# 64-row score products and q picks, and value products behind the half step, in a four-layer transformer kernel

## The chip, the cores and the metric

One NeuronCore of one Trainium2 chip runs the whole program in one launch. The metric is the device time of that core in microseconds (us), the median of three runs.

## The reference, cut to what matters

Sixteen sequences of 512 tokens with 512 features pass through four layers, each behind a layer norm and with a residual: a delta-rule attention, a feed-forward layer with a top-2 LoRA, a softmax attention with a linear memory, and the feed-forward layer again. The change lies in the third layer:

```python
qh = q.reshape(b, s, N_QUERY, N_HEAD, D_HEAD)      # 4 x 8 = 32 heads of 16 features
kh = k.reshape(b, s, N_HEAD, D_HEAD)               # 8 key/value heads
scores = jnp.einsum('bsqhd,bthd->bqhst', qh, kh) * scale
probs = jax.nn.softmax(scores, axis=-1)
a_dot = jnp.einsum('bqhst,bthd->bsqhd', probs, vh)
sigma_q = jax.nn.elu(q.reshape(b, s, N_QUERY, D_KV))
a_mem = sigma_q @ memory / (sigma_q @ memory_norm)
out = a_dot * (1.0 - w) + a_mem * w
```

## The kernel before

The program has two parts, one after the other. `delta_rule_layer` does the first layer of all sequences, some 2.8 ms; `token_layers` does the other three, one sequence after another (16 passes of a loop body that is unrolled twice), some 227 us each. The change touches `token_layers` alone.

In its attention the scores are needed twice. Once with the queries on the partitions, to find each query's maximum (`maximum(g, st)`, called M below: head g, query tile st of 128): TensorE writes 128 x 512 scores into one of three PSUM banks, and VectorE reduces them to one column (`tensor_reduce`, line 1586). Once with the keys on the partitions (`score(h, tt)`, called S: head h, key tile tt): TensorE writes them into one of three other banks, with the maximum already taken off, and ScalarE takes the exponential into `probs` (line 1140). Both products are float32r matmuls of 512 columns. A head has only 16 features, split in parts that are stacked: 48 rows of products and one row for the shift, in a block of 64 rows. `q_stack` holds two heads per tile, the even one in rows 0 to 63 and the odd one in rows 64 to 127. `k_stack` holds one tile for each of the 8 key heads, with zeros in the 64 rows of the other parity, so that a contraction over all 128 rows gives one head. The zeros are made by the scale and bias columns `head_rows` in `k_pair` (VectorE for pairs 0 and 2, ScalarE for 1 and 3, two instructions for each pair).

The stacks are made by selection products: `pick_k` (lines 1248 and 1249, a hi and a lo product of 32 rows each, from another 32-row block for each pair) and `pick_q(m)` (lines 1275 and 1276, a hi and a lo product of 128 rows, where only 32 rows of `sel` aren't zero), each copied out by `k_pair` or by ScalarE's `q_pair`.

The order on TensorE is written out by hand. Step g of 45 has two half steps j. In each stands, as far as it applies: up to two q picks (g below 7), M(g, 2j), at j = 1 of every fourth step four transposes of the maxima (line 1360, called maxT, which become the shift), S(g-7, 2j), a value block, M(g, 2j+1), S(g-7, 2j+1), and the products with the memory (line 1290). The value block (`values`, line 1333, called V) is one key tile of four heads: four plain float32 matmuls, 128 rows by 32 columns each, side by side. Four heads make a quad and have four value blocks, in the half steps that `AV_SLOTS` names: j = 1 of steps 4n+3, 4n and 4n+1 (V0 to V2), j = 0 of step 4n+2 (V3). At the end of every fourth step (4n+3) the finished quad is transposed (line 1380, called turn), VectorE normalises it (lines 1576 and 1580) ahead of its next maximum, and the next maxT waits for that, since both use bank 7.

The order of the others follows. ScalarE takes the exponentials in order; the first one of head h (h of 7 and more) waits for `av_mm`, that is for the last value block of the quad whose `probs` buffer it overwrites. M waits for the reduction three before it, S for the exponential three before it, and TensorE works off its queue in order. The first 7 to 8 steps have maxima and picks (called stretch A), steps up to 31 have maxima and scores (B), steps 32 to 38 scores alone (C), and then come the last value blocks.

Of the kernel before, what the change touches and what calls it, by code (L numbers as in the profile page):

```python
# [18 lines left out]
F32R = mybir.dt.float32r  # L19
# [4 lines left out]
P = 128  # L24
# [816 lines left out]
def token_layers(nc, dims, x2_in, w_ffn, b_ffn, lora_b, gate_b, w_q, w_kv, mem_aug_in, mem_w_in, ident_in, rank_mask_in, sel_in, head_rows_in, out):  # L841
# [3 lines left out]
    with ExitStack() as ctx:  # L845
        def sb(name, shape, dt=F32):
            return ctx.enter_context(nc.sbuf_tensor(name, shape, dt))
# [29 lines left out]
        sel = sb("sel", [P, 2 * HP + 2, P], F32R)  # L877
        head_rows = sb("head_rows", [P, 2, 2])

# [14 lines left out]
        q_stack = sb("q_stack", [P, NQ * NKV // 2, SEQ], F32R)  # L895
        k_stack = sb("k_stack", [P, NKV, SEQ], F32R)
        v_aug = sb("v_aug", [P, NT, NKV, 32])
# [151 lines left out]
        def _(act):  # L1049
# [4 lines left out]
            act.wait_ge(c_in, 112)  # L1054
            act.activation(mem_w[:, :], mem_w[:, :], ACT.Tanh, scale=0.5).then_inc(mem_tanh, 1)

            def norm_hi(b, f):
# [5 lines left out]
            with act.Fori(0, NBATCH // 2) as bb:  # L1063
                for par in range(2):
# [30 lines left out]
                    def k_pair(m):  # L1095

                        act.wait_ge(ksel_mm, at(b, HP, m + 1))
                        for e in range(2):
                            last = act.activation(k_stack[:, 2 * m + e, :], ps[:, m % STACK_BANKS, :], ACT.Identity,
                                                  bias=head_rows[:, e, 1:2], scale=head_rows[:, e, 0:1])  # L1100
                        last.then_inc(kodd_ready, 1)

# [57 lines left out]
        def _(pe):  # L1160
# [23 lines left out]
            with pe.Fori(0, NBATCH // 2) as bb:  # L1184
                for par in range(2):
# [84 lines left out]
                    def pick_q(m):  # L1270
                        n, hp = divmod(m, HP)
                        if hp == 0:
                            pe.wait_ge(qlo_ready, at(b, NQ, n + 1))
                        bank = stack_bank(HP + m)
                        pe.matmul(ps[:, bank, :], sel[:, hp, :], q_hi[:, n, :], start=True, stop=False)  # L1275
                        pe.matmul(ps[:, bank, :], sel[:, HP + hp, :], q_lo[:, n, :], start=False, stop=True).then_inc(qsel_mm, 1)  # L1276

# [16 lines left out]
                    def pair(h):  # L1294

                        n, kv = divmod(h, NKV)
                        return n * HP + kv // 2, kv

                    def maximum(g, st):

                        qt, kv = pair(g)
                        m = NT * g + st
                        if m in (1, 2):
                            pe.wait_ge(qrelu_ready, at(b, NQ, m))
                            pe.wait_ge(qlo_ready, at(b, NQ, m))
                        elif m >= MAX_BANKS:
                            pe.wait_ge(max_ready, at(b, NT * NH, m - MAX_BANKS + 1))
                        pe.matmul(ps[:, STACK_BANKS + m % MAX_BANKS, :], q_stack[:, qt, P * st:P * st + P], k_stack[:, kv, :],  # L1308
                                  start=True, stop=True).then_inc(max_mm, 1)

                    def score(h, tt):

                        qt, kv = pair(h)
                        if h == 0 and tt == 0:
                            pe.wait_ge(qstack_ready, at(b, NQ * HP, NQ * HP))
                        if h % 4 == 0 and tt == 0:
                            pe.wait_ge(shift_in, at(b, 64 * QUADS, 64 * (h // 4 + 1)))
                        m = NT * h + tt
                        if m >= STACK_BANKS:
                            pe.wait_ge(exp_ready, at(b, NT * NH, m - STACK_BANKS + 1))  # L1320
                        pe.matmul(ps[:, m % STACK_BANKS, :], k_stack[:, kv, P * tt:P * tt + P], q_stack[:, qt, :],  # L1321
                                  start=True, stop=True).then_inc(score_mm, 1)
# [15 lines left out]
                    for g in range(NH + OUT_LAG):  # L1338
                        h = g - SCORE_LAG
                        for j in range(2):  # L1340
# [21 lines left out]
                            if 0 <= h < NH:  # L1362
                                score(h, 2 * j)
                            quad, i = divmod(g - 3 - AV_LAG, 4)
                            if (i, j) in AV_SLOTS and 0 <= quad < QUADS:
                                values(quad, AV_SLOTS.index((i, j)))
                            if g < NH:
                                maximum(g, 2 * j + 1)
                            if 0 <= h < NH:
                                score(h, 2 * j + 1)  # L1370
                            if j == 0 and 0 <= g - MEM_LAG < NT:
                                memory(g - MEM_LAG)
# [15 lines left out]
        def _(dve):  # L1388
# [11 lines left out]
            dve.wait_ge(dve_consts, 2)  # L1400
            dve.wait_ge(c_in, 112)
            dve.wait_ge(pool_consts, 3)
            dve.wait_ge(w_hi_done, 5)
# [45 lines left out]
            with dve.Fori(0, NBATCH // 2) as bb:  # L1449
                for par in range(2):  # L1450
# [86 lines left out]
                    def k_pair(m):  # L1537

                        dve.wait_ge(ksel_mm, at(b, HP, m + 1))
                        for e in range(2):  # L1540
                            last = dve.tensor_scalar(k_stack[:, 2 * m + e, :], ps[:, m % STACK_BANKS, :], head_rows[:, e, 0:1], head_rows[:, e, 1:2],
                                                     ALU.mult, ALU.add)
                        last.then_inc(keven_ready, 1)

# [134 lines left out]
```

## Time and profile before

| | us |
|---|---|
| median of 3 runs (lowest, highest) | 6420.12 (6418.07, 6423.28) |
| the profiled execution's own time | 6432.57 |
| its span | 6430.8 |
| TensorE matmuls busy | 5567.4 (87%) |
| VectorE busy | 3720.7 (58%) |
| ScalarE busy | 2422.5 (38%) |
| GpSimd busy | 909.5 (14%) |
| mean granted TensorE clock | 0.836 of full |

### The profile page before, as it was taken

How to read it: one execution, taken by the hardware profiler on the slowest of the kernel's cores; microseconds unless marked ns; L12 is line 12 of the kernel's file. 1: busy time of each engine (PE TensorE's matmuls, PEld its weight loads, DVE VectorE, ACT ScalarE, POOL GpSimd, SP SyncE). 2: the span in 40 equal slices, each digit the busy share in tenths (PEclk: the TensorE clock that was granted, in tenths of full speed). 3: DMA queues.
4: the chain of work that ended last, by engine and by line, in shares of the span. 5: the costliest groups of instructions: out<-in, count | busy, mean ns of one | idle time of the engine just before them, and what ended most of it. 6: DMA issues, size and time to landing. Idle time of an engine off the chain costs nothing.

```text
span 6430.8 us, 154830 instructions
## 1 busy us (share of the span) xinstructions
PE 5567.4 (87%) x62928; PEld 4184.4 (65%) x62928; DVE 3720.7 (58%) x7900; ACT 2422.5 (38%) x4497; POOL 909.5 (14%) x1075
## 2 busy tenths in 40 slices
PE   4899888889888988859889988988898899889888
PEld 4788787778777888745655565555556555555655
DVE  3555555555555555526756665665566567566656
ACT  2222222222222222216435534544554454345345
POOL 0111111111111111111111121112112111210111
PEclk8777776777777777669999989999999999899899
DMA  2111111111111111110000000000000000000000
GB/s 62 43 46 44 43 45 49 49 48 49 49 49 42 46 44 43 45 54 1 14 14 14 1 15 14 1 15 14 15 1 14 15 1 14 14 14 1 15 14 8
DMA packets 352479, 173.53 MB, mean 27 GB/s; under 512 B 300016, under 2 KB 300784, under 8 KB 350992
## 3 DMA queue, kind: packets, MB, share of 16 engines
q1 hardware_dynamic: 343056, 146.25, 8.5%
q10 hardware_dynamic: 8704, 16.78, 0.8%
q8 instruction: 562, 9.21, 0.6%
q14 instruction: 157, 1.29, 0.1%
HBM read 94.27 MB, written 67.63 MB: 25 GB/s over the span
## 4 chain that ended last, share of the span: by engine, by line
issue 27%; PE 19%; DVE 6%; POOL 3%; ACT 1%; DMA 0%; DVEq 0%; POOLq 0%; SPq 0%; ACTq 0%
PE row_psum L40 5%; PE row_psum L42 4%; PE row_psum L41 4%; DVE smax L1586 2%; POOL xs L1042 1%; PE row_psum L1171 1%; PE row_psum L1308 1%; DVE stats L1412 1%; PE row_psum L1275 1%; POOL rstd L1014 1%; PE row_psum L1276 1%; PE row_psum L1290 1%; DVE xr_lo L1441 0%; DVE xs L1515 0%; DVE probs L1423 0%
## 5 line engine op out<-in xcount | busy, mean ns | idle before, releaser
L1586 DVE TENSOR_REDUCE smax<-row_psum 128x1 f32<-128x512 f32 x2048 | 1279.5, 683 | 306.9 <-PE row_psum L1308 305.9
L1140 ACT ACTIVATE probs<-row_psum 128x512 f32<-128x512 f32 x2048 | 1109.1, 602 | 505.2 <-PE row_psum L1321 401.2
L1308 PE MATMUL row_psum<-k_stack,q_stack 128*128 128x512 f32 x2048 | 872.4, 437 | 28.2 <-DVE smax L1586 24.5
L1321 PE MATMUL row_psum<-q_stack,k_stack 128*128 128x512 f32 x2048 | 837.2, 423 | 22.3 <-ACT probs L1140 13.8
L1308 PEld LDWEIGHTS row_psum<-k_stack,q_stack 128*128 128x128 f32 x2048 | 394.5, 193 | 462.1 <-DVE smax L1586 388.3
L529 PE MATMUL span_bank<-rhs,inv_b 32*32 32x64 f32 x8192 | 441.8, 303 | 150.0 <-issue 84.3
L1333 PE MATMUL row_psum<-probs,v_aug 128*32 128x512 f32 x4096 | 538.9, 604 | 9.2 <-ACT av_sb L1153 9.2
L1321 PEld LDWEIGHTS row_psum<-q_stack,k_stack 128*128 128x128 f32 x2048 | 380.3, 191 | 254.3 <-ACT probs L1140 198.0
L529 PEld LDWEIGHTS span_bank<-rhs,inv_b 32*32 32x32 f32 x8192 | 424.0, 166 | 160.4 <-issue 160.4
L708 DVE TENSOR_TENSOR lane_t<-lane_t,lane_p 128x30 f32<-128x30 f32 (+14 forms) x960 | 408.6, 426 | 33.0
L723 DVE TENSOR_TENSOR tri<-span_bank,masks 128x512 f32<-128x512 f32 x256 | 156.0, 682 | 383.1 <-PE span_bank L509 383.1
L40 PE MATMUL row_psum<-wf_hi,xr_hi 128*128 128x320 f32 (+1 forms) x1024 | 335.4, 328 | 31.9 <-issue 17.7
L705 DVE TENSOR_TENSOR lane_p<-lane_t 128x30 f32<-128x30 f32 (+14 forms) x960 | 340.0, 354 | 30.8
L41 PE MATMUL row_psum<-wf_lo,xr_hi 128*128 128x320 f32 (+1 forms) x1024 | 331.9, 324 | 0.0
L42 PE MATMUL row_psum<-wf_hi,xr_lo 128*128 128x320 f32 (+1 forms) x1024 | 331.5, 324 | 0.0
L1171 PE MATMUL row_psum<-ident,probs 128*128 128x128 f32 x784 | 167.5, 368 | 177.5 <-DVE probs L1423 177.5
L1042 POOL TENSOR_TENSOR xs<-xs,av_n 128x256 f32<-128x256 f32 x128 | 93.1, 727 | 1549.7 <-DVE av_n L1580 1549.7
L40 PE MATMUL span_bank<-x_hi,w_hi 128*128 128x256 f32 x1024 | 299.0, 292 | 3.0 <-DVE x_lo L687 3.0
L732 DVE TENSOR_TENSOR rhs<-rhs,span_bank 128x512 f32<-128x512 f32 x128 | 82.3, 684 | 364.4 <-PE span_bank L529 364.4
L41 PE MATMUL span_bank<-x_lo,w_hi 128*128 128x256 f32 x1024 | 287.6, 281 | 0.0
L42 PE MATMUL span_bank<-x_hi,w_lo 128*128 128x256 f32 x1024 | 287.2, 281 | 0.0
L1171 PEld LDWEIGHTS row_psum<-ident,probs 128*128 128x128 f32 x784 | 117.7, 184 | 226.3 <-DVE probs L1423 176.1
(203 smaller groups left out, 10609.0 us busy)
## 6 DMA issues: line engine op xcount, KB each, us to landing
xs<-x SPq DMA_DIRECT2D x17, 1024.0 KB, 5.6
x_sp<-in_x ACTq DMA_DIRECT2D x32, 512.0 KB, 3.3
tri_dram<-tri SPq DMA_DIRECT2D x256, 64.0 KB, 2.3
lane_t<-tri_dram SPq DMA_DIRECT2D x32, 512.0 KB, 3.4
inv_dram<-lane_t SPq DMA_DIRECT2D x32, 512.0 KB, 2.6
inv_b<-inv_dram SPq DMA_DIRECT2D x256, 64.0 KB, 2.3
x_res<-in_x SPq DMA_DIRECT2D x32, 512.0 KB, 4.5
x<-x_res SPq DMA_DIRECT2D x32, 512.0 KB, 2.8
```

Source lines behind the costliest of these rows:

```text
L40: pe.matmul(out, a_hi, b_hi, start=first, stop=False)
L41: pe.matmul(out, a_hi, b_lo, start=False, stop=False)
L42: return pe.matmul(out, a_lo, b_hi, start=False, stop=last)
L529: last = pe.matmul(bank[4 + 2 * t + h // 8][dst:dst + NB, 2 * HD * (h % 8):2 * HD * (h % 8) + 2 * HD], weights(h, src), moving(src, h), st ...
L705: mark(dve.tensor_tensor(prod, lane_t[:, 0:m, m:m + 1].to_broadcast([P, m, n]), lane_t[:, m:m + 1, m + 1:NB].to_broadcast([P, m, n]), ALU. ...
L708: mark(dve.tensor_tensor(lane_t[:, 0:m, m + 1:NB], lane_t[:, 0:m, m + 1:NB], prod, ALU.add))
L1140: act.activation(probs[:, h % PROBS, tt, :], ps[:, m % STACK_BANKS, :], ACT.Exp, scale=float(DH) ** -0.5).then_inc(exp_ready, 1)
L1171: last = pe.transpose(ps[:, t, P * k:P * k + P], xn[:, t, P * k:P * k + P], ident2[:, :])
L1308: pe.matmul(ps[:, STACK_BANKS + m % MAX_BANKS, :], q_stack[:, qt, P * st:P * st + P], k_stack[:, kv, :], start=True, stop=True).then_inc(m ...
L1321: pe.matmul(ps[:, m % STACK_BANKS, :], k_stack[:, kv, P * tt:P * tt + P], q_stack[:, qt, :], start=True, stop=True).then_inc(score_mm, 1)
L1333: last = pe.matmul(ps[32 * e:32 * e + 32, 6, :], v_aug[:, tt, h % NKV, :], probs[:, h % PROBS, tt, :], start=tt == 0, stop=tt == NT - 1)
L1586: dve.tensor_reduce(smax[:, g, st:st + 1], ps[:, STACK_BANKS + (NT * g + st) % MAX_BANKS, :], AX.X, ALU.max).then_inc(max_ready, 1)
```

## The change

`k_stack` gets one tile for a pair of key heads, the even in rows 0 to 63 and the odd in rows 64 to 127, without zeros; `k_pair` becomes one instruction for each pair, which adds a column of ones in the two shift rows (`shift_ones`, made once at the start, for which ScalarE and VectorE wait once). `maximum` and `score` contract over the 64 rows of their head, taken from both stacks. `pick_q` contracts over the 64 rows in which its selection lies. And the value block stands behind the second M and S of its half step, no longer between the first S and the second M.

```diff
@@ -876,6 +876,7 @@
 
         sel = sb("sel", [P, 2 * HP + 2, P], F32R)
         head_rows = sb("head_rows", [P, 2, 2])
+        shift_ones = sb("shift_ones", [P, 1])
 
 
         xs = sb("xs", [P, 2, NT, D])
@@ -893,7 +894,7 @@
         xat_hi = sb("xat_hi", [P, SEQ], F32R)
         xat_lo = sb("xat_lo", [P, SEQ], F32R)
         q_stack = sb("q_stack", [P, NQ * NKV // 2, SEQ], F32R)
-        k_stack = sb("k_stack", [P, NKV, SEQ], F32R)
+        k_stack = sb("k_stack", [P, HP, SEQ], F32R)
         v_aug = sb("v_aug", [P, NT, NKV, 32])
         smax = sb("smax", [P, NQ * NKV, NT])
         shift = sb("shift", [4, SEQ], F32R)
@@ -1053,6 +1054,7 @@
                 act.activation(d2, stage[:, 0:size], ACT.Copy).then_inc(w_hi_done, 1)
             act.wait_ge(c_in, 112)
             act.activation(mem_w[:, :], mem_w[:, :], ACT.Tanh, scale=0.5).then_inc(mem_tanh, 1)
+            act.wait_ge(dve_consts, 3)
 
             def norm_hi(b, f):
                 for t in range(NT):
@@ -1095,10 +1097,8 @@
                     def k_pair(m):
 
                         act.wait_ge(ksel_mm, at(b, HP, m + 1))
-                        for e in range(2):
-                            last = act.activation(k_stack[:, 2 * m + e, :], ps[:, m % STACK_BANKS, :], ACT.Identity,
-                                                  bias=head_rows[:, e, 1:2], scale=head_rows[:, e, 0:1])
-                        last.then_inc(kodd_ready, 1)
+                        act.activation(k_stack[:, m, :], ps[:, m % STACK_BANKS, :], ACT.Identity,
+                                       bias=shift_ones[:, 0:1]).then_inc(kodd_ready, 1)
 
                     def q_pair(m):
                         act.wait_ge(qsel_mm, at(b, NQ * HP, m + 1))
@@ -1272,8 +1272,9 @@
                         if hp == 0:
                             pe.wait_ge(qlo_ready, at(b, NQ, n + 1))
                         bank = stack_bank(HP + m)
-                        pe.matmul(ps[:, bank, :], sel[:, hp, :], q_hi[:, n, :], start=True, stop=False)
-                        pe.matmul(ps[:, bank, :], sel[:, HP + hp, :], q_lo[:, n, :], start=False, stop=True).then_inc(qsel_mm, 1)
+                        r = slice(64 * (hp // 2), 64 * (hp // 2) + 64)
+                        pe.matmul(ps[:, bank, :], sel[r, hp, :], q_hi[r, n, :], start=True, stop=False)
+                        pe.matmul(ps[:, bank, :], sel[r, HP + hp, :], q_lo[r, n, :], start=False, stop=True).then_inc(qsel_mm, 1)
 
                     pick_q(0)
 
@@ -1294,23 +1295,24 @@
                     def pair(h):
 
                         n, kv = divmod(h, NKV)
-                        return n * HP + kv // 2, kv
+                        e = kv % 2
+                        return n * HP + kv // 2, kv // 2, slice(64 * e, 64 * e + 64)
 
                     def maximum(g, st):
 
-                        qt, kv = pair(g)
+                        qt, hp, rows = pair(g)
                         m = NT * g + st
                         if m in (1, 2):
                             pe.wait_ge(qrelu_ready, at(b, NQ, m))
                             pe.wait_ge(qlo_ready, at(b, NQ, m))
                         elif m >= MAX_BANKS:
                             pe.wait_ge(max_ready, at(b, NT * NH, m - MAX_BANKS + 1))
-                        pe.matmul(ps[:, STACK_BANKS + m % MAX_BANKS, :], q_stack[:, qt, P * st:P * st + P], k_stack[:, kv, :],
+                        pe.matmul(ps[:, STACK_BANKS + m % MAX_BANKS, :], q_stack[rows, qt, P * st:P * st + P], k_stack[rows, hp, :],
                                   start=True, stop=True).then_inc(max_mm, 1)
 
                     def score(h, tt):
 
-                        qt, kv = pair(h)
+                        qt, hp, rows = pair(h)
                         if h == 0 and tt == 0:
                             pe.wait_ge(qstack_ready, at(b, NQ * HP, NQ * HP))
                         if h % 4 == 0 and tt == 0:
@@ -1318,7 +1320,7 @@
                         m = NT * h + tt
                         if m >= STACK_BANKS:
                             pe.wait_ge(exp_ready, at(b, NT * NH, m - STACK_BANKS + 1))
-                        pe.matmul(ps[:, m % STACK_BANKS, :], k_stack[:, kv, P * tt:P * tt + P], q_stack[:, qt, :],
+                        pe.matmul(ps[:, m % STACK_BANKS, :], k_stack[rows, hp, P * tt:P * tt + P], q_stack[rows, qt, :],
                                   start=True, stop=True).then_inc(score_mm, 1)
 
                     def values(quad, tt):
@@ -1361,13 +1363,13 @@
                                 last.then_inc(maxT_mm, 1)
                             if 0 <= h < NH:
                                 score(h, 2 * j)
-                            quad, i = divmod(g - 3 - AV_LAG, 4)
-                            if (i, j) in AV_SLOTS and 0 <= quad < QUADS:
-                                values(quad, AV_SLOTS.index((i, j)))
                             if g < NH:
                                 maximum(g, 2 * j + 1)
                             if 0 <= h < NH:
                                 score(h, 2 * j + 1)
+                            quad, i = divmod(g - 3 - AV_LAG, 4)
+                            if (i, j) in AV_SLOTS and 0 <= quad < QUADS:
+                                values(quad, AV_SLOTS.index((i, j)))
                             if j == 0 and 0 <= g - MEM_LAG < NT:
                                 memory(g - MEM_LAG)
                         quad, i = divmod(g - 3 - TURN_LAG, 4)
@@ -1399,6 +1401,8 @@
             dve.tensor_scalar(mem_w[:, :], mem_w[:, :], 0.5, 0.5, ALU.mult, ALU.add).then_inc(dve_consts, 1)
             dve.wait_ge(dve_consts, 2)
             dve.wait_ge(c_in, 112)
+            dve.tensor_tensor(shift_ones[:, :], head_rows[:, 0, 1:2], head_rows[:, 1, 1:2], ALU.add).then_inc(dve_consts, 1)
+            dve.wait_ge(dve_consts, 3)
             dve.wait_ge(pool_consts, 3)
             dve.wait_ge(w_hi_done, 5)
             own = [0]
@@ -1537,10 +1541,8 @@
                     def k_pair(m):
 
                         dve.wait_ge(ksel_mm, at(b, HP, m + 1))
-                        for e in range(2):
-                            last = dve.tensor_scalar(k_stack[:, 2 * m + e, :], ps[:, m % STACK_BANKS, :], head_rows[:, e, 0:1], head_rows[:, e, 1:2],
-                                                     ALU.mult, ALU.add)
-                        last.then_inc(keven_ready, 1)
+                        dve.tensor_scalar(k_stack[:, m, :], ps[:, m % STACK_BANKS, :], shift_ones[:, 0:1], None,
+                                          ALU.add).then_inc(keven_ready, 1)
 
                     def elu_exp(n):
 

```

## Rows read from the trace of the kernel before

**Rows 1.** The page's costliest groups: count, then busy us and mean ns, idle before.

```profile
L1586 DVE TENSOR_REDUCE smax<-row_psum 128x1 f32<-128x512 f32 x2048 | 1279.5, 683 | 306.9 <-PE row_psum L1308 305.9
L1140 ACT ACTIVATE probs<-row_psum 128x512 f32<-128x512 f32 x2048 | 1109.1, 602 | 505.2 <-PE row_psum L1321 401.2
L1308 PE MATMUL row_psum<-k_stack,q_stack 128*128 128x512 f32 x2048 | 872.4, 437 | 28.2 <-DVE smax L1586 24.5
L1333 PE MATMUL row_psum<-probs,v_aug 128*32 128x512 f32 x4096 | 538.9, 604 | 9.2 <-ACT av_sb L1153 9.2
```

**Rows 2.** A stretch: length, busy PE, PEld, DVE, ACT, POOL (counts); PEclk, DMA share, GB/s.

```profile
3165.60:3232.90 67.30, 67.21 (x363) 35.08 (x362) 53.02 (x90) 47.73 (x91) 2.91 (x4) 1.00 0.01 2
```

**Rows 3.** Timeline of VectorE, one quad: start us, us, instruction, idle before.

```profile
3193.30 1.88 DVE L1586 TENSOR_REDUCE smax<-row_psum 128x1 f32<-128x512 f32 x3
3195.93 2.48 DVE L1586 TENSOR_REDUCE smax<-row_psum 128x1 f32<-128x512 f32 x4 [0.75 <-PE row_psum L1308]
3198.97 1.29 DVE L1586 TENSOR_REDUCE smax<-row_psum 128x1 f32<-128x512 f32 x2 [0.55 <-PE row_psum L1308]
3201.09 3.68 DVE L1586 TENSOR_REDUCE smax<-row_psum 128x1 f32<-128x512 f32 x6 [0.83 <-PE row_psum L1308]
3205.40 0.69 DVE L1586 TENSOR_REDUCE smax<-row_psum 128x1 f32<-128x512 f32 x1 [0.63 <-PE row_psum L1308]
...
3206.70 1.88 DVE L1586 TENSOR_REDUCE smax<-row_psum 128x1 f32<-128x512 f32 x3
```

**Rows 4.** Timeline of TensorE's matmuls, same quad.

```profile
3196.89 0.39 PE L1308 MATMUL row_psum<-k_stack,q_stack 128*128 128x512 f32 x1
3197.12 0.39 PE L1321 MATMUL row_psum<-q_stack,k_stack 128*128 128x512 f32 x1
3197.43 1.06 PE L1333 MATMUL row_psum<-probs,v_aug 128*32 128x512 f32 x8
3198.43 0.50 PE L1308 MATMUL row_psum<-k_stack,q_stack 128*128 128x512 f32 x1
3198.77 0.39 PE L1321 MATMUL row_psum<-q_stack,k_stack 128*128 128x512 f32 x1
...
3205.44 0.60 PE L1380 MATMUL row_psum<-ident,av_sb 128*128 128x128 f32 x4
3205.79 0.48 PE L1308 MATMUL row_psum<-k_stack,q_stack 128*128 128x512 f32 x1
```

**Rows 5.** Timeline of TensorE's matmuls, around the first three k picks.

```profile
3115.53 0.51 PE L1248 MATMUL row_psum<-xat_hi,sel 32*128 32x512 f32 x3
3115.87 0.40 PE L1249 MATMUL row_psum<-xat_lo,sel 32*128 32x512 f32 x3
3116.20 0.50 PE L40 MATMUL row_psum<-xr_hi,wq_hi 128*128 128x512 f32 x1
```

**Rows 6.** Timeline of TensorE's weight loads, a maximum that waited for its bank.

```profile
3202.43 0.19 PEld L1308 LDWEIGHTS row_psum<-k_stack,q_stack 128*128 128x128 f32 x1 [0.19 <-DVE smax L1586]
```

**Rows 7.** Timeline of ScalarE, behind V3 of the same quad.

```profile
3200.75 1.17 ACT L1140 ACTIVATE probs<-row_psum 128x512 f32<-128x512 f32 x2 [0.95 <-PE row_psum L1333]
3201.82 0.59 ACT L1153 ACTIVATE av_sb<-row_psum 128x512 f32<-128x512 f32 x1
3202.29 2.57 ACT L1140 ACTIVATE probs<-row_psum 128x512 f32<-128x512 f32 x5
```

**Rows 8.** Stretches of 5 us, columns as in rows 2.

```profile
2010.00:2015.00 5.00, 5.00 (x104) 5.00 (x102) 1.28 (x2) 0.18 (x1) 0.00 (x0) 0.50 0.00 0
...
3155.00:3160.00 5.00, 4.21 (x14) 3.34 (x15) 3.12 (x6) 2.73 (x5) 1.28 (x1) 0.66 0.00 0
...
3240.00:3245.00 5.00, 4.39 (x20) 1.88 (x20) 0.03 (x1) 4.46 (x9) 0.00 (x0) 1.00 0.01 2
```

**Rows 9.** Timeline of VectorE, at the start of stretch B.

```profile
3157.89 0.69 DVE L1586 TENSOR_REDUCE smax<-row_psum 128x1 f32<-128x512 f32 x1 [0.16 <-PE row_psum L1308]
```

**Rows 10.** Timeline of ScalarE, set-up, behind the last q projection.

```profile
3122.98 1.09 ACT L1093 ACTIVATE xr_hi<-row_psum 128x512 fp32r<-128x512 f32 x2 [1.24 <-PE row_psum L42]
```

## Prediction, made before the changed kernel ran

> **What bounds the kernel now.** I read the page's groups first. In `token_layers` the costliest are the maxima, their reductions, the exponentials and the value blocks. VectorE sits idle 306.9 us ahead of its 2048 reductions, nearly all of it waiting for M, ScalarE 505.2 us ahead of the exponentials, most of it for S, while TensorE waits 28.2 us ahead of M [rows 1]. So in this attention TensorE sets the pace. Next I asked where. In one sequence's stretch with maxima, scores and value blocks, from 3165.60 to 3232.90, TensorE is busy 67.21 of 67.30 us at clock 1.00, VectorE 53.02 and ScalarE 47.73 [rows 2]. That leaves VectorE 14.3 us idle; over 16 sequences 228 us, the ceiling of a gain here.
>
> The timelines of one quad give the period and its parts. The quad takes 3206.70 - 3193.30 = 13.40 us. Reductions that aren't held up follow each other every 0.60 us (four in 2.48, the last record 0.69). The normalisation adds 3206.70 - 3205.40 - 0.69 = 0.61. VectorE thus needs 16 x 0.60 + 0.61 = 10.2 us, and loses 3.2 in four gaps of 0.55 to 0.83 [rows 3]. On TensorE M to S is 0.23 us. Around a value block S to V is 0.31, V to M 1.00 and M to S 0.34, in all 1.65 where two slots would be 0.46: a block costs 1.19. The turn costs 0.35 [rows 4], maxT is alike. Sum: 32 x 0.23 + 4 x 1.19 + 2 x 0.4 = 12.9, with short waits 13.4. TensorE bound.
>
> **The change part by part.**
>
> *64-row products.* M of head g and S of head g-7 lie always in opposite halves of the rows, since 7 is odd. Can they run side by side? The three k picks of 32 rows, each in its own row block, show it: their three hi matmuls begin within one record of 0.51 us, the three lo ones 0.34 later, and the next product 0.33 after that. Six matmuls take 0.67 us; in line they would take 6 x 0.23 = 1.4 [rows 5]. So row blocks do overlap, in this number format. Picks wait for no semaphore between them, M and S do; that is the part not shown. Bounds for a pair M, S: 0.23 (full overlap) and 0.46 (none). I take 0.23, by the nearest row. TensorE's quad is then 16 x 0.23 + 4 x 1.19 + 1.2 (turn and maxT with their changes of shape) = 9.6 us, below VectorE's 10.2. The bound moves to VectorE and to how the blocks interrupt it.
>
> *What is late next.* M may go once the reduction three before is over: 0.69 after that one's start plus 0.05 (a reduction that began at about 3201.69 lets the weight load go at 3202.43 [rows 6]), so 0.74. From M with its weight load to the reduction's start it is 3198.97 - 3198.43 = 0.54. Three reductions last 1.80, so M has 1.80 - 0.74 - 0.54 = 0.52 us of slack. A value block behind a pair: 0.11 for the pair's weight load (M to S behind a block is 0.34, not 0.23), 0.31 to V, 1.00 to the next M: 1.42, where 0.60 + 0.52 = 1.12 is free of cost. VectorE idles 0.3 us for each of V1, V2 and V3. V0 is followed at once by the turn, for whose end VectorE's normalisation waits: turn at 1.42, over at 2.02, while VectorE would be free at 1.66: 0.4. V3 now stands behind the second S, and the first exponential of the next head waits for V3. Already ScalarE waits 0.95 for it [rows 7]. Behind V3 ScalarE has five exponentials and the copy (3201.82 to 3202.29 is 0.47, the exponentials 0.51 each) before it gives the bank that the S ahead of V0 needs: 5 x 0.51 + 0.47 + 0.14 = 3.2 us, where VectorE's pace would want that S 2.5 behind V3. So V0 starts 0.7 late, and VectorE pays it. Idle in a quad 0.9 + 0.4 + 0.7 = 2.0, with a repeated hold-up at V2 to V3 (only four maxima apart less two) 2.1: quad 12.3 us instead of 13.4. The stretch holds 67.3 / 13.4 = 5.0 quads: 5.5 us a sequence. Bounds of this term: 0 (no overlap) and 14.3 (all idle gone).
>
> *Position of V in stretch C.* No maxima are left there, ScalarE's order sets the pace, and S of one head can't overlap its own kind (same half). V3 comes one S later, 0.23 us, and ScalarE waits for it: twice, -0.5 us. Bounds: -1 and 0.
>
> *Start of B.* The clock is 0.66 in mean there [rows 8], and VectorE waits 0.16 before each reduction, 0.85 apart, since M and S take 0.43 each [rows 9]. Three such gaps go when they overlap: +0.5. Bounds 0 and 1.
>
> *k_pair.* Two fewer instructions each on VectorE and ScalarE, about 1.5 us a sequence and engine. Worth nothing: TensorE's q projections run on meanwhile, and ScalarE has waited 1.24 us for the last of them before it takes q over [rows 10]. The same cover holds the one constant and its wait at the start. If that cover were gone it would give up to 1.5 a sequence.
>
> *q picks.* The rows of the contraction don't shorten a matmul. Some picks now fall in the other half than their neighbour M. Stretch A is bound by VectorE apart from its first steps: 0, bounds -1 (below) and +1.
>
> *Changes of shape.* S to V is 0.31 against 0.23 between equal shapes, and the first after a change loads its weights uncovered, 0.11 [rows 4]: 0.1 to 0.2 for each change. New are two around each maxT and each memory block and one at each turn, some 32 a sequence. Most fall where VectorE or ScalarE sets the pace: those at turn and maxT are in the 9.6 above; elsewhere 0.2 a sequence, bounds 0 and 5.
>
> The Trainium skill ("TensorEngine Tiling (Array Packing)", Key Properties) says that changing the tiling mode drains the engine; this speaks against the change where it adds such changes, and the 0.31 against 0.23 agrees with it. By that rule alone the sum stays, as the drain is in the row's price.
>
> *Clock.* In the delta layer TensorE is busy 5.00 of 5.00 us with 32 x 32 tiles, and the granted clock is 0.50 [rows 8]. So being busy isn't enough; parts of the array seem to count less. In stretch C the clock holds at 1.00 with full-row scores and value blocks [rows 8]; it will have 64-row scores there, and in A 64-row maxima and picks. What would one fall cost? A value block's 1.00 us would be 1.87 (0.43 / 0.23), so 0.87 for each block that is caught, and in A next to nothing for M and picks, which have slack, some 0.3 for a step. Bounds 0 and 14 (half of the 32 blocks). I take two blocks caught in a sequence and a step of A: -2.0 us.
>
> The Trainium skill ("TensorE: Matmul & The Clock Gate", Why this matters for your kernels) asks only for no long pauses between matmuls; by that the clock term would be 0 and the sum 85 us instead of 53. The row of the delta layer doesn't agree with it, so I keep the term.
>
> Sum per sequence: 5.5 - 0.5 + 0.5 - 0.2 - 2.0 = 3.3 us, times 16 = 53 us. The profiled execution took 6432.57 us, span 6430.8; it would take 6380. The median of the runs is 12.45 lower, which I carry over: 6367.
>
> **Rivals.**
>
> 1. *The blocks are hidden better.* If ScalarE's chain behind V3 doesn't reach V0 and the clock holds: idle in a quad 1.3, quad 11.5, 1.9 x 5 = 9.5 a sequence, 152 us: 6268; with one of the two alone some 6320. For it: ScalarE needs only 47.73 of 67.30 us [rows 2]. Against: it waits for V3 by a fixed order [rows 7]. I name 6300.
>
> 2. *The clock falls (slower).* Half-array matmuls leave TensorE at 1.2 GHz for much of the attention. Place: every value block caught there, price 0.87 each. Gains without the clock are 5.3 a sequence, so from 6 caught blocks of 32 the change loses. At 9 blocks: 7.8 + 1.0 in A = 8.8, net -3.5, times 16 = 56: 6476. For it: clock 0.50 at full busy in the delta layer. Against: value blocks and overlapped pairs fill the whole array, and C holds 1.00 now with S only every 0.51 us [rows 8].
>
> 3. *M and S don't overlap*, because each waits for its own semaphore, so the change doesn't do what it could. The quad stays 13.4 plus three changes of shape, 0.5, and the later V3: 5 x 0.5 + 0.5 = 3.0 a sequence, at most: 6420 to 6468. Against it the picks [rows 5].
>
> **How the numbers follow.** My forecast (6340 to 6405 by itself) has a chance of 0.60, rival 1 0.20, rival 2 0.14, rival 3 0.06. Range: from between rival 1 and its end, 6280, to 6440, which leaves out the bulk of rival 2. About 0.2%, 13 us, can be told from no change. Faster: 0.48 of the forecast and all of rival 1, 0.68. Within 0.2%: 0.12 of the forecast (a clock term of some 5) and 0.02 each of the others, 0.16. Slower: 0.12 and 0.04, 0.16.
>
> **What would show it.** The profile after should show M and S starting within 0.15 us of each other, a quad of about 12.3 us, VectorE waiting behind V and the turn rather than between, and ScalarE still waiting for V3, longer than 0.95. TensorE's stretch B should be no longer all busy. The windows of A and C tell the clock term: at 1.00 throughout rival 1 is nearer, below 0.8 rival 2. If starts of M and S stay 0.23 apart, the main step is wrong.

## The result and the profile after

The changed kernel takes 6565.62 us (6547.28 to 6590.44, 4 runs) beside 6421.70 before (4 runs): a ratio of 1.0225, 95% interval [1.0204, 1.0245]. It is 144 us slower; the forecast was 53 us faster. The profiled execution took 6561.14 us, span 6559.3, mean granted clock 0.788 where it was 0.836.

The page's groups of the changed kernel, as in [rows 1]:

```profile
L1588 DVE TENSOR_REDUCE smax<-row_psum 128x1 f32<-128x512 f32 x2048 | 1273.6, 683 | 211.8 <-PE row_psum L1310 209.7
L1140 ACT ACTIVATE probs<-row_psum 128x512 f32<-128x512 f32 x2048 | 1073.1, 613 | 608.4 <-PE row_psum L1323 353.8
L1310 PE MATMUL row_psum<-k_stack,q_stack 64*128 64x512 f32 x2048 | 905.8, 518 | 49.3 <-DVE smax L1588 43.2
L1335 PE MATMUL row_psum<-probs,v_aug 128*32 128x512 f32 x4096 | 622.3, 690 | 5.9 <-ACT av_sb L1153 5.9
```

VectorE waits 95 us less for the maxima. But most of that comes back at the turn. Its wait ahead of the reciprocal of the normalisation, first before, then after:

```profile
L1576 DVE RECIPROCAL av_rc<-row_psum 128x16 f32<-128x16 f32 x128 | 33.0, 258 | 376.6 <-PE row_psum L1380 376.6
L1578 DVE RECIPROCAL av_rc<-row_psum 128x16 f32<-128x16 f32 x128 | 33.0, 257 | 620.3 <-PE row_psum L1382 620.3
```

All idle time of VectorE inside stretch B together went from 236 to 206 us, so the gain is there, but it is 30 us. ScalarE waits 103 us more, and a record of a value product lasts 690 ns instead of 604, one of a maximum 518 instead of 437, though none has more columns. Matmuls that get longer without more work point to the clock.

Next, TensorE's matmuls in an undisturbed quad of the changed kernel:

```profile
3198.34 1.06 PE L1335 MATMUL row_psum<-probs,v_aug 128*32 128x512 f32 x8
3199.34 0.66 PE L1382 MATMUL row_psum<-ident,av_sb 128*128 128x128 f32 x4
3199.92 0.49 PE L1310 MATMUL row_psum<-k_stack,q_stack 64*128 64x512 f32 x1
3199.93 0.49 PE L1323 MATMUL row_psum<-q_stack,k_stack 64*128 64x512 f32 x1
3200.26 0.39 PE L1310 MATMUL row_psum<-k_stack,q_stack 64*128 64x512 f32 x1
3200.26 0.39 PE L1323 MATMUL row_psum<-q_stack,k_stack 64*128 64x512 f32 x1
```

M and S start within 0.01 us of each other, where they stood 0.23 apart [rows 4]. They overlap fully, although each has its own wait for a semaphore. V0 and the turn stand one behind the other, and the next maximum comes 1.58 us behind V0's start. VectorE in the same quad, and ScalarE behind V3:

```profile
3187.72 2.48 DVE L1588 TENSOR_REDUCE smax<-row_psum 128x1 f32<-128x512 f32 x4
3190.79 2.48 DVE L1588 TENSOR_REDUCE smax<-row_psum 128x1 f32<-128x512 f32 x4 [0.59 <-PE row_psum L1310]
3193.50 1.29 DVE L1588 TENSOR_REDUCE smax<-row_psum 128x1 f32<-128x512 f32 x2 [0.23 <-PE row_psum L1310]
3195.15 3.69 DVE L1588 TENSOR_REDUCE smax<-row_psum 128x1 f32<-128x512 f32 x6 [0.36 <-PE row_psum L1310]
3200.03 0.26 DVE L1578 RECIPROCAL av_rc<-row_psum 128x16 f32<-128x16 f32 x1 [1.20 <-PE row_psum L1382]
...
3200.67 2.47 DVE L1588 TENSOR_REDUCE smax<-row_psum 128x1 f32<-128x512 f32 x4
```

```profile
3194.81 1.08 ACT L1140 ACTIVATE probs<-row_psum 128x512 f32<-128x512 f32 x2 [1.93 <-PE row_psum L1335]
```

The quad takes 12.95 us (3200.67 - 3187.72) against 13.40 [rows 3]; most other quads at full clock take 12.82. VectorE waits 0.2 to 0.6 behind the blocks and 1.20 for the turn; ScalarE's wait for V3 is 1.93 instead of 0.95 [rows 7].

Then the stages of one sequence, first before, then after. The four rows are stretch A (to the first maximum of step 7), steps 7 to 10, stretch B from step 11 to the last maximum, and C with the last value blocks; columns as in [rows 2]:

```profile
3126.59:3149.08 22.49, 19.83 (x83) 13.58 (x83) 20.80 (x39) 11.51 (x21) 2.97 (x3) 0.94 0.01 1
3149.08:3163.31 14.23, 11.58 (x51) 8.30 (x49) 12.19 (x26) 8.12 (x16) 3.38 (x3) 0.88 0.01 2
3163.31:3232.23 68.92, 68.83 (x370) 35.36 (x369) 54.22 (x93) 48.79 (x93) 2.91 (x4) 1.00 0.01 2
3232.23:3258.58 26.35, 23.42 (x137) 8.46 (x135) 2.72 (x8) 17.38 (x33) 2.18 (x3) 1.00 0.01 1
```

```profile
3116.72:3143.09 26.37, 23.98 (x85) 16.51 (x83) 20.94 (x40) 11.01 (x20) 3.50 (x3) 0.56 0.01 1
3143.09:3156.78 13.69, 10.91 (x47) 7.28 (x46) 11.98 (x25) 7.64 (x16) 2.83 (x3) 0.75 0.01 2
3156.78:3225.80 69.02, 65.41 (x365) 25.07 (x366) 54.00 (x92) 47.40 (x93) 2.90 (x4) 0.92 0.01 2
3225.80:3263.72 37.92, 34.98 (x145) 11.33 (x144) 2.69 (x9) 17.18 (x34) 2.19 (x3) 0.70 0.01 1
```

The clock is 0.56 in A and 0.70 in C, where it was 0.94 and 1.00, though TensorE is busy for no smaller share: 91% of A (23.98 of 26.37) after 88%, 92% of C after 89%. In C the same value blocks take 1.94 us each, where one took 1.06 before [rows 4]:

```profile
3245.12 1.94 PE L1335 MATMUL row_psum<-probs,v_aug 128*32 128x512 f32 x8
3246.99 2.27 PE L1323 MATMUL row_psum<-q_stack,k_stack 64*128 64x512 f32 x4
3249.19 1.94 PE L1335 MATMUL row_psum<-probs,v_aug 128*32 128x512 f32 x8
```

To see all sequences, I took from each trace the starts of the 1st, 29th, 45th and 128th reduction and of the last reciprocal of every sequence. The means over the sequences in us, with the time at 1.2 GHz in brackets ("rest" is all else of a sequence, of which there are 15 intervals):

```
                A             7 to 10       B             C             rest
before          22.44 ( 2.4)  13.72 (1.9)   68.99 (0.0)   26.36 ( 0.0)  92.12
after           25.08 (19.8)  13.55 (6.0)   66.80 (6.0)   35.14 (16.0)  92.13
v_move          22.53 ( 2.6)  14.25 (3.6)   69.81 (0.0)   29.89 ( 3.0)  91.83
rows_only       25.09 (19.9)  13.55 (6.0)   65.23 (1.9)   32.85 (16.2)  91.96
b_only_vold     22.27 ( 1.8)  13.75 (6.6)   66.60 (5.5)   26.29 ( 0.0)  91.95
b_only_vnew     22.40 ( 2.2)  13.69 (6.5)   68.30 (9.3)   29.96 ( 3.0)  91.89
c64             22.54 ( 2.7)  14.04 (3.0)   68.97 (0.0)   28.52 ( 5.1)  91.62
a64             36.11 (31.1)  14.39 (3.4)   68.95 (0.0)   26.37 ( 0.0)  91.67
picks64         35.37 (30.2)  14.72 (4.8)   69.00 (0.0)   26.37 ( 0.0)  91.86
c_shadow        25.91 (22.0)  13.63 (5.9)   66.92 (6.2)   29.88 ( 1.9)  91.07
b11             22.29 ( 1.7)  13.87 (2.3)   64.49 (0.0)   26.30 ( 0.0)  91.62
b11_mix         22.26 ( 1.7)  14.02 (2.8)   64.62 (0.0)   26.29 ( 0.0)  91.60
v0_move         22.59 ( 3.0)  13.85 (2.3)   68.29 (0.0)   27.32 ( 0.2)  92.06
v3_move         22.45 ( 2.3)  13.93 (2.6)   70.85 (0.0)   27.22 ( 0.9)  91.49
```

Before to after: A +2.64, 7 to 10 -0.17, B -2.19, C +8.78, together +9.06 a sequence, 145 us over 16. That is the difference of the medians; the rest, with the copies of `k_pair`, is unchanged. The two profiled executions differ by 128.5 us only, because all that lies ahead of the first maximum took 17 us less in that of the changed kernel (2890.7 against 2907.9), which the change hardly touches; over all kernels here it took 2883 to 2908.

### The profile page after: what moved, and what is told of

Same layout as the page of the kernel before. It is cut to its first block, busy times and chain, and to the rows that moved or that the text cites. A ratio compares the mean times of both kernels' runs of the same rounds, so it can differ in the third digit from the quotient of the medians.

```text
span 6559.3 us, 154769 instructions
## 1 busy us (share of the span) xinstructions
PE 5656.7 (86%) x62928; PEld 4057.9 (62%) x62928; DVE 3691.7 (56%) x7869; ACT 2367.0 (36%) x4465; POOL 908.8 (14%) x1075
## 4 chain that ended last, share of the span: by engine, by line
issue 27%; PE 19%; DVE 7%; POOL 3%; ACT 1%; DMA 0%; DVEq 0%; POOLq 0%; SPq 0%
PE row_psum L40 5%; PE row_psum L41 4%; PE row_psum L42 4%; DVE smax L1588 3%; POOL xs L1043 1%; PE row_psum L1171 1%; PE row_psum L1310 1%; PE row_psum L1291 1%; DVE stats L1416 1%; POOL rstd L1015 1%; PE row_psum L1276 1%; DVE xr_lo L1445 0%; PE row_psum L1277 0%; DVE xs L1519 0%; DVE probs L1427 0%
## 5 line engine op out<-in xcount | busy, mean ns | idle before, releaser
L1140 ACT ACTIVATE probs<-row_psum 128x512 f32<-128x512 f32 x2048 | 1073.1, 613 | 608.4 <-PE row_psum L1323 353.8
L1323 PE MATMUL row_psum<-q_stack,k_stack 64*128 64x512 f32 x2048 | 897.1, 507 | 62.2 <-ACT probs L1140 42.2
L1310 PE MATMUL row_psum<-k_stack,q_stack 64*128 64x512 f32 x2048 | 905.8, 518 | 49.3 <-DVE smax L1588 43.2
L1310 PEld LDWEIGHTS row_psum<-k_stack,q_stack 64*128 64x128 f32 x2048 | 415.1, 218 | 439.6 <-DVE smax L1588 386.2
L1335 PE MATMUL row_psum<-probs,v_aug 128*32 128x512 f32 x4096 | 622.3, 690 | 5.9 <-ACT av_sb L1153 5.9
L1323 PEld LDWEIGHTS row_psum<-q_stack,k_stack 64*128 64x128 f32 x2048 | 374.1, 204 | 396.2 <-ACT probs L1140 246.1
L1578 DVE RECIPROCAL av_rc<-row_psum 128x16 f32<-128x16 f32 x128 | 33.0, 257 | 620.3 <-PE row_psum L1382 620.3
L40 PE MATMUL row_psum<-wf_hi,xr_hi 128*128 128x320 f32 (+1 forms) x1024 | 336.4, 329 | 32.1 <-issue 17.3
```

The source lines that it names most:

```text
L40: pe.matmul(out, a_hi, b_hi, start=first, stop=False)
L1140: act.activation(probs[:, h % PROBS, tt, :], ps[:, m % STACK_BANKS, :], ACT.Exp, scale=float(DH) ** -0.5).then_inc(exp_ready, 1)
L1310: pe.matmul(ps[:, STACK_BANKS + m % MAX_BANKS, :], q_stack[rows, qt, P * st:P * st + P], k_stack[rows, hp, :], start=True, stop=True).then ...
L1323: pe.matmul(ps[:, m % STACK_BANKS, :], k_stack[rows, hp, P * tt:P * tt + P], q_stack[rows, qt, :], start=True, stop=True).then_inc(score_m ...
L1335: last = pe.matmul(ps[32 * e:32 * e + 32, 6, :], v_aug[:, tt, h % NKV, :], probs[:, h % PROBS, tt, :], start=tt == 0, stop=tt == NT - 1)
```

## Experiments

Theory 1, the clock: half-array products let TensorE fall to 1.2 GHz where no full-array work stands beside them, in A and C. Theory 2, the order: V3 and the turn come too late. Theory 3: the changes of shape, or the overlap itself, cost the time. Each ratio is against the kernel before, run again beside the experiment. The edits are shown shortened.

**The two parts apart.** `v_move` is the kernel before with only this edit:

```diff
-  values(quad, AV_SLOTS.index((i, j)))     # between score(h, 2j) and maximum(g, 2j + 1)
+  values(quad, AV_SLOTS.index((i, j)))     # behind score(h, 2j + 1)
```

> The kernel before with one part of the change: the value block behind the second M and S of its half step, all products over 128 rows. Clock theory (half-array products leave TensorE at 1.2 GHz in stretches A and C): this part is worth nearly nothing, 0 to +0.5 us a sequence, 6420 to 6430 us, mean clock as before (0.836). Order theory (V3 and the turn come too late, ScalarE waits 1.93 us instead of 0.95 for V3): most of the loss is here, above 6480 us at an unchanged clock.

Measured: 6498.27 us, ratio 1.0111 [1.0086, 1.0136], 73 us slower. Theory 1 alone fails here: the move carries half of the loss. The time is theory 2's, the clock not quite: in 14 of 16 sequences stretch C has 3.4 us at 1.2 GHz, though all products have full rows, and takes 30.1 us; in the other two it takes 28.5, against 26.4 before. `rows_only` is the changed kernel with this edit taken back.

> The changed kernel with the value block back in its old place; 64-row maxima, scores and picks remain. Clock theory: as slow as the changed kernel, 6540 to 6570 us, clock near 0.79. Order theory: faster than before, below 6420 us, since the overlap of M and S is kept and the late V3 is gone.

Measured: 6507.66 us, ratio 1.0132 [1.0103, 1.0161], 82 us slower. `v_move` came out within theory 2's time, `rows_only` within neither: each theory holds about one half, 73 + 82 = 155 for 144. The table places them. The rows cost 2.65 us in A and 6.49 in C and give 3.76 in B, where most quads take 12.53 us. In the one sequence of `rows_only` whose stretch C stays at full clock, C takes 26.29 us; in the other fifteen it has 13.7 or 20.5 us at 1.2 GHz and takes 31.9 to 34.5. The move costs 1.6 in B and 2.3 in C on top, in B with 6.0 us at 1.2 GHz where `rows_only` has 1.9.

**64 rows only where M and S stand together.** `k_stack` keeps its zeros, so that the contraction can be chosen for each product:

```diff
+  def rows_of(h, half):
+      return slice(64 * (h % 2), 64 * (h % 2) + 64) if half else slice(0, P)
...
+  r = rows_of(g, g >= 7)                   # in maximum; in score: rows_of(h, h + 7 < NH)
-  pe.matmul(..., q_stack[:, qt, P * st:P * st + P], k_stack[:, kv, :], ...)
+  pe.matmul(..., q_stack[r, qt, P * st:P * st + P], k_stack[r, kv, :], ...)
```

> 64 rows only where maxima and scores stand together (maxima of steps 7 to 31, scores of heads 0 to 24); maxima of steps 0 to 6, scores of heads 25 to 31 and all picks over 128 rows, k_stack as before with its zeros, value block in its old place. Clock theory: stretches A and C keep their clock, the gain of B stays, 0.5 to 1.1 us for each of 5 quads: 6335 to 6385 us, mean clock above 0.82. Theory that the changes of shape or the overlap itself cost the time: slower than before, above 6430 us, as B holds them all.

> As b_only_vold, with the value block behind the second M and S. Clock theory: nearly the same as b_only_vold, up to 1 us a sequence slower for the later V3: 6340 to 6400 us. Order theory: slower than before, and over 5 us a sequence slower than b_only_vold.

Measured: `b_only_vold` 6374.50 us, ratio 0.9923 [0.9895, 0.9950], faster than before; `b_only_vnew` 6480.78, ratio 1.0092 [1.0067, 1.0117]. A and C are back at 22.3 and 26.3 us. 100 of the 128 maxima and of the 128 scores of a sequence still overlap and change shape, so theory 3 falls for stretch B. With the late value blocks the same kernel is 106 us slower, so theory 2 holds for that part: C is 3.7 us longer and B 1.7, though B also has 9.3 us at 1.2 GHz instead of 5.5.

**One stretch alone.** Three kernels with one condition each: scores of the last seven heads over 64 rows (`rows_of(h, h + 7 >= NH)`), maxima of steps 0 to 6 (`rows_of(g, g < 7)`), q picks over 64 rows.

> The kernel before, where the scores of the last seven heads (stretch C, no maxima beside them) contract over 64 rows and nothing else is changed. Nothing can overlap there, and no product gets longer. Clock theory: the clock falls in C, value blocks there take 1.9 us instead of 1.0, 4 to 8 us a sequence: 6480 to 6550 us. If rows don't matter for the clock: 6415 to 6430 us.

> The kernel before, where the maxima of steps 0 to 6 alone (stretch A) contract over 64 rows. Clock theory: half of A at 1.2 GHz, 1 to 3 us a sequence: 6435 to 6470 us. If rows don't matter for the clock: 6415 to 6430 us.

> The kernel before with the q picks over 64 rows, nothing else. Clock theory: part of A at 1.2 GHz, 0 to 2 us a sequence: 6420 to 6455 us. If rows don't matter for the clock: 6410 to 6430 us.

Measured: `c64` 6458.31 us, ratio 1.0069 [1.0052, 1.0086]; `a64` 6635.18, ratio 1.0331 [1.0310, 1.0353]; `picks64` 6641.93, ratio 1.0357 [1.0338, 1.0377]. All slower, the first less than expected, the other two far more, so all three miss the ranges of the clock theory and only its direction holds. In `c64` one trace holds both outcomes of the same instructions. Two sequences' stretch C, then value blocks from each:

```profile
3216.00:3242.36 26.36, 23.07 (x137) 7.83 (x135) 2.71 (x8) 17.39 (x33) 2.19 (x3) 1.00 0.01 2
3444.00:3476.10 32.10, 29.02 (x137) 9.25 (x135) 2.72 (x8) 17.41 (x33) 2.18 (x3) 0.79 0.01 1
```

```profile
3226.64 1.06 PE L1339 MATMUL row_psum<-probs,v_aug 128*32 128x512 f32 x8
...
3229.54 1.07 PE L1339 MATMUL row_psum<-probs,v_aug 128*32 128x512 f32 x8
...
3455.00 1.93 PE L1339 MATMUL row_psum<-probs,v_aug 128*32 128x512 f32 x8
...
3460.21 1.93 PE L1339 MATMUL row_psum<-probs,v_aug 128*32 128x512 f32 x8
```

Clock 1.00: 26.4 us, to the tenth as before. Clock 0.79: 32.1. Nine of the sixteen sequences are of the first kind, seven took 29.2 to 32.1. The shape of the scores costs nothing in itself; what counts is whether the clock falls. In `a64` it falls for nearly all of A: in the sequence shown A is at 0.55, and TensorE, with 64-row maxima between 128-row picks, is busy for 36.64 of 37.05 us. The timeline of its matmuls:

```profile
3135.36 1.22 PE L1313 MATMUL row_psum<-k_stack,q_stack 64*128 64x512 f32 x2
3136.51 0.79 PE L1275 MATMUL row_psum<-xr_hi,sel 128*128 128x512 f32 x1
3137.10 0.63 PE L1276 MATMUL row_psum<-xr_lo,sel 128*128 128x512 f32 x1
3137.66 1.22 PE L1313 MATMUL row_psum<-k_stack,q_stack 64*128 64x512 f32 x2
```

Two maxima and a pick take 2.30 us (3137.66 - 3135.36). The kernel before has the same order in one shape, in 3.4 us at 1.2 GHz at the start of A, from pick to pick 1.71 us (3128.49 - 3126.78):

```profile
3126.78 0.63 PE L1275 MATMUL row_psum<-xr_hi,sel 128*128 128x512 f32 x1
...
3128.49 0.63 PE L1275 MATMUL row_psum<-xr_hi,sel 128*128 128x512 f32 x1
```

VectorE's pace would be 1.2. So the halved clock makes TensorE the bound of stretch A, and the changes of shape add 0.6 us to each such group on top. The changed kernel has M and picks both at 64 rows, which spares it that, and some of them overlap there: A is 25.1, not 36. How much each of the two spares wasn't tested.

**More work, less time.** The sharpest test of theory 1 adds work to the changed kernel:

```diff
   pe.matmul(ps[:, m % STACK_BANKS, :], k_stack[rows, hp, ...], q_stack[rows, qt, :], ...)
+  if h + SCORE_LAG > NH:
+      if h + SCORE_LAG == NH + 1 and tt == 0:
+          pe.wait_ge(max_ready, at(b, NT * NH, NT * NH))
+      other = slice(64 - rows.start, 128 - rows.start)
+      pe.matmul(ps[:, STACK_BANKS + h % 2, :], k_stack[other, hp, ...], q_stack[other, qt, :], ...)
```

> The changed kernel with extra work in stretch C: from step 33 on each score product is followed by a second 64-row product of the other half of the same stacks, into a spare PSUM bank that nobody reads. It takes no part in the result. Clock theory: it runs beside the score, fills the array, the clock stays at 2.4 GHz in C, and C falls from 35.1 us to about 30 (where the late value block alone leaves it): 70 to 90 us faster than the changed kernel, 6475 to 6500 us. If the loss in C comes from the shape changes or from the waits of 64-row products, more work can't help: 6560 us or more.

Measured: 6494.79 us, as theory 1 expected, 71 us less than the changed kernel, ratio to the kernel before 1.0098 [1.0081, 1.0115] where the changed kernel has 1.0225. Stretch C went from 35.14 to 29.88 us, its time at 1.2 GHz from 16.0 to 1.9. The added product starts with the score and costs nothing:

```profile
3246.98 0.49 PE L1323 MATMUL row_psum<-q_stack,k_stack 64*128 64x512 f32 x1
3246.98 0.49 PE L1329 MATMUL row_psum<-q_stack,k_stack 64*128 64x512 f32 x1
```

The shapes and the order of all other products are the same, with 24 idle products and one wait more a sequence: theory 1 is shown for C. Longer pauses aren't the cause here: over the sixteen stretches C TensorE is busy for 89% of the time before, 92% in the changed kernel and 89% in `c_shadow`, and its longest single pause there is 0.72 to 0.73 us in all three. What is left over 26.36 is the late block: `v_move` without any 64-row product has 29.89. For A no run fills the array. There theory 1 rests on the rows taken away and given back: the clock falls with half rows in one shape (`rows_only`) and in mixed shapes (`a64`, `picks64`), and with full rows A is as before (`b_only_vold`).

**Which value block.** V0 alone moved, and V3 alone moved, both in the kernel before.

> The kernel before, where only V0 of each quad stands behind the second M and S. V0 then runs straight into the turn. Merged-turn theory: it carries most of what the move of all four costs (73 us): 6460 to 6500 us. ScalarE theory (V3 is what matters): 6415 to 6435 us.

> The kernel before, where only V3 of each quad stands behind the second M and S, so that ScalarE's first exponential of the next head waits longer for it. ScalarE theory: it carries most of the 73 us of the whole move: 6460 to 6500 us, ScalarE's wait for V3 1.2 us or more instead of 0.95. Merged-turn theory: 6415 to 6435 us.

Measured: `v0_move` 6434.43 us, ratio 1.0003 [0.9994, 1.0013], no change: B gains 0.7 and C loses 1.0. `v3_move` 6450.09, ratio 1.0053 [1.0036, 1.0070], 29 us slower and in neither range. The run into the turn is not it. V3 matters, by the time less than expected: ScalarE waits 1.41 instead of 0.95 for it, as its timeline shows,

```profile
3172.22 1.09 ACT L1140 ACTIVATE probs<-row_psum 128x512 f32<-128x512 f32 x2 [1.41 <-PE row_psum L1339]
```

and in `v_move`, with all four moved, 2.53:

```profile
3193.95 1.08 ACT L1140 ACTIVATE probs<-row_psum 128x512 f32<-128x512 f32 x2 [2.53 <-PE row_psum L1339]
```

In stretch B V3 alone is enough: at full clock most quads take 13.4 us before and in `v0_move`, and 13.8 in both `v3_move` and `v_move`. But 0 and 29 don't make 73. By the table most of what is missing lies in C, where all four moves together cost 3.5 us a sequence and V0 and V3 alone 1.0 and 0.9. At full clock C takes 28.5 us in `v_move`, 27.2 in `v0_move` and 26.8 in `v3_move`, after 26.4 before, and 3.4 us at 1.2 GHz, which `v_move` has in 14 sequences, add 1.6 each time. Whether V1 and V2 do the rest or the moves together, no run tells, and it stays open.

**A better kernel.** 64 rows only from step 11 on (`g >= 11`, `11 <= h + 7 < NH`), where value blocks stand, and in `b11_mix` full rows again in the two half steps between V3 and V0. All else as before.

> As b_only_vold, but 64 rows only from step 11 on, where the first value block stands; steps 7 to 10 are full again. Clock theory: the fall to 1.2 GHz in steps 7 to 11 (6.6 us a sequence in b_only_vold, 1.9 before) goes, which is worth up to 1 us a sequence: 6355 to 6375 us. Otherwise as b_only_vold, 6375 us.

> As b11, with full rows also in the two half steps of every quad that lie between its value blocks V3 and V0 and have none. Clock theory: stretch B keeps 2.4 GHz throughout (5.5 us at 1.2 GHz in b_only_vold), TensorE has room there: 6340 to 6365 us. Theory that changes of shape (two more a quad) cost more than the clock: slower than b11, above 6380 us.

Measured: `b11` 6344.42 us, ratio 0.9875 [0.9858, 0.9891], 87 us faster than before and 221 than the changed kernel; `b11_mix` 6357.90, ratio 0.9887 [0.9871, 0.9904]. `b11` is better than its expected range, which counted only on steps 7 to 10: the 5.5 us at 1.2 GHz that `b_only_vold` had in B are gone too, and B falls from 66.60 to 64.49 us. B is at clock 1.00 in both, so `b11_mix` has nothing to mend; their intervals overlap. One sequence of `b11`, the four stages:

```profile
3112.50:3135.26 22.76, 20.08 (x81) 13.69 (x81) 20.53 (x39) 11.92 (x22) 2.69 (x3) 0.93 0.01 1
3135.26:3149.39 14.13, 11.48 (x52) 8.38 (x51) 12.18 (x25) 7.87 (x17) 3.65 (x3) 0.88 0.01 2
3149.39:3213.88 64.49, 62.42 (x370) 24.50 (x369) 54.20 (x92) 48.48 (x94) 2.90 (x4) 1.00 0.01 2
3213.88:3240.19 26.31, 23.42 (x138) 8.51 (x136) 2.65 (x7) 17.38 (x33) 2.18 (x3) 1.00 0.01 2
```

B is 4.5 us shorter, the other stages stand as before. 4.5 x 16 = 72 of the 87 us. The others lie where nothing was changed (the rest of a sequence and the part ahead of the first maximum), in which kernels here differ by as much.

## Why the prediction was wrong

Forecast: +3.3 us gained a sequence. Measured: 9.1 lost. Step by step:

- *What bounds the kernel, and the overlap*: right. TensorE set the pace of B, M and S overlap fully (0.01 us apart), and VectorE and the blocks set it now.
- *What is late next*: right in kind, 0.5 to 0.6 too good. Quad 12.3 forecast, 12.82 to 12.95 measured at full clock. The hold-up at V0 and the turn was forecast as 0.4 + 0.7, and is 1.20. At V1, which shares its half step with the maxT, a gap of 0.5 to 0.6 stands where 0.3 was forecast; the other two are 0.2 and 0.4. All idle in the quad shown is 2.38 (0.59 + 0.23 + 0.36 + 1.20) for 2.1 forecast. The larger miss is VectorE's own work, taken as 10.2: the four gaps in [rows 3] add up to 2.76, not to the 3.2 that the prediction subtracted, so its own rows gave 13.40 - 2.76 = 10.6, and 12.95 - 2.38 = 10.6 is what the quad has now. With 6.0 us of B at 1.2 GHz, B gave 2.2, not 5.5.
- *Position of V in stretch C*: mis-sized. Forecast 0.5 a sequence, measured 2.3 in C on top of the 64 rows (35.14 - 32.85), and 2.2 at full clock without them (28.5 against 26.35, `v_move`). The forecast counted only V3's delay; V3 alone costs 0.5 in C at full clock and V0 alone 0.9, which had no term. Why the four moves cost more together isn't shown.
- *Start of B*: forecast 0.5, measured 0.2. *k_pair*: nothing, as forecast (rest 92.12 and 92.13). *Changes of shape*: forecast 0.2; in C at full clock nothing is to be seen of them (26.36 in `c64`, 26.35 before), while `a64` shows that at 1.2 GHz in a mixed stretch they do not stay hidden.
- *Clock*: the step that failed. The direction and the evidence were right (the delta layer's 5.00 us busy at clock 0.50 [rows 8]), the size was not: 2.0 us a sequence forecast, 9.1 measured (A 2.65 and C 6.49 of `rows_only`), inside the bounds of 0 and 14 but far from the value taken. I counted single caught blocks. In fact A is at 1.2 GHz for 19.9 us of 25.1 and C for 16.2 of 32.9 (`rows_only`): the fall is the state of the stretch, not an accident of single blocks. The price of a block was right (1.94 against 1.06 is 0.88, forecast 0.87), but in stretch C of the changed kernel shown above five are caught, not two, and the scores between them, four in 2.27 us, are slow as well and had no price.

The kernel went as rival 2, and the sign named for it came: the clock is below 0.8 in A and C. Rival 2 put 9 caught blocks at 56 us; with the misplaced value blocks it came to 144. It got a chance of 0.14, though the only row on small tiles in this trace (clock 0.50 at full busy) spoke for it, and what spoke against it was an argument and a row of full-row scores.

The Trainium skill ("TensorE: Matmul & The Clock Gate", Why this matters for your kernels) ties the clock to pauses between matmuls. `c_shadow`, with pauses as long (at most 0.72 us in C, 0.73 in the changed kernel) and the array filled, runs 71 us faster than the changed kernel, so here the measurement decides against that as the whole rule.

## What to carry to other kernels

Splitting a contraction into row halves pays where two independent products stand side by side, as here M and S with value blocks between them; where a half stands alone it saved nothing here, and it halved the clock of everything around it for long stretches, so try the padded full-row product there. Look at the granted clock by stage before and after, and read a longer matmul of the same shape as a clock that fell. When a block is moved in a hand-written order, follow which engine waits for its last instruction by a fixed order: a later V3 cost more than it freed.

## What the runs showed of the hardware

- The granted clock follows how much of the array works, not only how long TensorE is busy. C of the kernel before, with full-row scores: 1.00 in all 16 sequences. With 64-row scores and nothing else changed (`c64`): 1.00 in nine, down to 0.79 in the others. With a second 64-row product beside each in the changed kernel: 16.0 us at 1.2 GHz become 1.9. Rows of zeros keep the clock up too: the kernel before has them in half of the rows of `k_stack`, at 1.00.
- The rows aren't all: `v_move`, with full rows everywhere and only the value blocks later, has 3.4 us at 1.2 GHz in C in 14 of 16 sequences.
- Two 64-row float32r matmuls in opposite halves, each with its own semaphore wait, start within 0.01 us of each other in the changed kernel, and a record of each lasts 0.39 us, as one alone does.
- TensorE can be busy without a break and stay at 1.2 GHz: in `a64` stretch A is at it for 31.1 of 36.1 us in mean, and TensorE is busy for 36.64 of 37.05 us of one such stretch.
